# Graph-attention layer: where VectorE's mask and TensorE's scores stand in a step, and who adds the mask

## The reference

```python
h = relu(layernorm(x))                                   # x [4096, 256]
neib_att = tanh(neigh @ Wn1 + bn1) @ Wn2 + bn2           # [4096, 32]
x_att    = tanh(h @ Wx1 + bx1) @ Wx2 + bx2               # [4096, 32]
value    = neigh @ Wv + bv                               # [4096, 128]
ws = leaky_relu(x_att @ neib_att.T, 0.01)                # [4096, 4096]
ws = where(adj > 0, ws, -9e15); ws = softmax(ws, axis=1)
out = x + concat([h @ Wfx + bfx, ws @ value], axis=1)
```

## Time and profile before

| | |
|---|---|
| median of 3 runs | 552.23 us (551.5 to 552.99) |
| time of the profiled execution | 552.71 us, its span 550.5 us |
| granted TensorE clock over the span | 0.983 |
| PE busy | 505.3 us, 92% |
| DVE busy | 478.2 us, 87% |
| ACT busy | 432.7 us, 79% |
| POOL busy | 211.8 us, 38% |
| HBM read and written | 154 GB/s over the span |

### The profile page before, as it was taken

How to read it: one execution, slowest core, us unless ns; L and a number is a source line. 1 busy time by engine, 2 the same in 40 slices (tenths; PEclk the granted TensorE clock), 3 DMA queues, 4 the chain that set the end, 5 groups by cost and what they waited for, 6 DMA issues and landing times.

```text
span 550.5 us, 8742 instructions
## 1 busy us (share of the span) xinstructions
PE 505.3 (92%) x2759; PEld 378.3 (69%) x2759; DVE 478.2 (87%) x883; ACT 432.7 (79%) x585; POOL 211.8 (38%) x325
## 2 busy tenths in 40 slices
PE   5798788899999999999999999999999999998996
PEld 4455556677777767766877677766777686776784
DVE  2669897999999999999999999999998999996664
ACT  2563688898888888888888878888888889897553
POOL 1402123234633654355434553456435444440100
PEclk8898999899999999999999999999999999999999
DMA  7752865454456545664356445643565445620100
GB/s 205 190 166 48 143 135 98 92 115 78 76 87 139 89 69 96 117 135 76 59 107 147 73 78 113 119 91 64 95 114 96 77 74 94 113 46 1 40 1 19
DMA packets 38013, 52.00 MB, mean 94 GB/s; under 512 B 3920, under 2 KB 29776, under 8 KB 37968
## 3 DMA queue, kind: packets, MB, share of 16 engines
q0 software_dynamic: 9216, 33.56, 37.5%
q1 hardware_dynamic: 28752, 17.90, 11.3%
HBM read 80.81 MB, written 4.19 MB: 154 GB/s over the span
## 4 chain that ended last, share of the span: by engine, by line
PE 34%; DVE 16%; issue 11%; ACT 11%; POOL 7%; DMA 3%; DVEq 1%; POOLq 0%; ACTq 0%
PE ps_turned L884 10%; POOL scores L421 6%; DVE pt_lo L655 5%; PE ps_scores L861 5%; PE ps_product L903 4%; PE ps_product L905 4%; PE ps_product L904 4%; ACT scores L512 4%; ACT scores L524 4%; DVE mask L642 4%; DVE scores L676 3%; PE ps_scores L860 3%; DMA adj_in<-in_adj 3%; ACT pt_hi L489 2%; PE ps_product L814 1%
## 5 line engine op out<-in xcount | busy, mean ns | idle before, releaser
L421 POOL TENSOR_TENSOR scores<-scores,mask 128x512 f32<-128x512 f32 x109 | 129.2, 1186 | 203.6 <-ACT scores L512 203.6
L655 DVE TENSOR_TENSOR pt_lo<-ps_turned,pt_hi 128x512 fp32r<-128x512 f32 x256 | 175.1, 685 | 32.1 <-ACT pt_hi L489 15.9
L489 ACT ACTIVATE pt_hi<-ps_turned 128x512 fp32r<-128x512 f32 x256 | 152.5, 597 | 55.6 <-PE ps_turned L884 49.5
L884 PE MATMUL ps_turned<-ident,scores 128*128 128x128 f32 x1024 | 158.3, 277 | 11.4 <-DVE pt_lo L655 11.0
L884 PEld LDWEIGHTS ps_turned<-ident,scores 128*128 128x128 f32 x1024 | 119.9, 141 | 61.3 <-DVE pt_lo L655 30.4
L512 ACT ACTIVATE scores<-ps_scores 128x1024 f32<-128x1024 f32 x128 | 131.1, 1025 | 28.7 <-PE ps_scores L861 25.9
L524 ACT ACTIVATE scores<-scores,neg_top 128x2048 f32<-128x2048 f32 x64 | 127.9, 1998 | 0.0
L676 DVE CUSTOM_DVE_ANT_0 scores<-ps_scores,scores,top 128x1024 f32<-128x1024 f32 x96 | 122.2, 1273 | 2.8 <-ACT scores L512 0.9
L903 PE MATMUL ps_product<-pt_hi,v_hi 128*128 128x512 f32 x256 | 113.1, 442 | 0.2 <-DVE pt_lo L655 0.2
L861 PE MATMUL ps_scores<-neib,xs 128*128 128x512 f32 x256 | 109.9, 507 | 0.0
L905 PE MATMUL ps_product<-pt_lo,v_hi 128*128 128x512 f32 x256 | 101.4, 396 | 0.0
(11 more groups left out here) (76 smaller groups left out, 385.1 us busy)
## 6 DMA issues: line engine op xcount, KB each, us to landing
adj_in<-in_adj POOLq DMA_DIRECT2D x64, 512.0 KB, 5.5
scores<-in_L_gnn_neigh SPq DMA_DIRECT2D x8, 512.0 KB, 4.3
x_rows<-in_x SPq DMA_DIRECT2D x8, 512.0 KB, 6.6
x_left<-in_x SPq DMA_DIRECT2D x8, 256.0 KB, 5.7
x_right<-in_x SPq DMA_DIRECT2D x8, 256.0 KB, 2.9
out_h<-x_left SPq DMA_DIRECT2D x8, 256.0 KB, 2.3
out_h<-x_right SPq DMA_DIRECT2D x8, 256.0 KB, 5.1
scores<-in_x SPq DMA_DIRECT2D x1, 512.0 KB, 5.0
```

Of the source, the lines that this page charges most:

```text
L421: pool.tensor_tensor(half, half, mask[:, s % 2, BANK:CHUNK], ALU.add).then_inc(masked, 1)
L489: act.activation(pt_hi[:, (2 * b + u) % HI_RING], pt[:, u], ACT.Copy).then_inc(hi_done, 1)
L655: dve.tensor_tensor(pt_lo[:, u], pt[:, u], pt_hi[:, (2 * b + u) % HI_RING].bitcast(FP32), ALU.subtract).then_inc(lo_done, 1)
L884: last = pe.transpose(pt[:, u, i * P:(i + 1) * P], scores[:, parity * TILES + i, n * P:(n + 1) * P], ident[:, :])
```

## The change

VectorE makes the masks two chunks ahead instead of one, in a ring of three buffers instead of two, and from step 19 as the last thing of its step. What was behind `lo(s, 1)` (negated maximum, sums, outputs, side work) now stands between the two `lo`. TensorE's scores come first in its step, ahead of `turn(s, 0)`. From step 19 no mask matmul is left: GpSimd adds both halves, as two instructions of 512 columns. The adjacency loads go out on even steps, with a wait for the same masks as before. The ring of `pt_hi` has three buffers instead of four. ScalarE's copy of a finished group comes ahead of `hi(s, 0)`. The last loop of SyncE that was not written out is written out.

```diff
-HI_RING = 4
+HI_RING = 3
+MASK_RING = 3
...
-        mask = sb("mask", [P, 2, CHUNK], BF16)
+        mask = sb("mask", [P, MASK_RING, CHUNK], BF16)
...
@@ GpSimd
-                    pool.wait_ge(risen, s + 1 + PERIOD * it)
-                    half = scores[:, parity * TILES + tile, c * CHUNK + BANK:(c + 1) * CHUNK]
-                    pool.tensor_tensor(half, half, mask[:, s % 2, BANK:CHUNK], ALU.add).then_inc(masked, 1)
-                n = s - LOAD + 1 + ADJ_RING
+                    pool.wait_ge(risen, s + 1)
+                    pool.wait_ge(mask_done, s + 1)
+                    for h in range(2):
+                        half = scores[:, parity * TILES + tile, c * CHUNK + h * BANK:c * CHUNK + (h + 1) * BANK]
+                        last = pool.tensor_tensor(half, half, mask[:, s % MASK_RING, h * BANK:(h + 1) * BANK], ALU.add)
+                    last.then_inc(masked, 1)
+                n = s - LOAD + 2 + ADJ_RING
                 if n % LOAD == 0 and ADJ_RING <= n < STEPS:
-                    pool.wait_ge(mask_done, s + 1 + PERIOD * it)
-                    load_adj(n, n // CHUNKS + 2 * TILES * it)
+                    pool.wait_ge(mask_done, n - ADJ_RING + LOAD)
+                    load_adj(n, n // CHUNKS)
...
@@ ScalarE
+            def step(s):
+                aggregate(s)
+                hi(s, 0)
+                rise(s)
+                hi(s, 1)
+                power(s)
+                side(s)
...
@@ VectorE
-                if it_is(it, e, NEIGH_GROUPS - 1):
-                    mask_of(0, 0)
+                if e == NEIGH_GROUPS - 1:
+                    for n in range(2):
+                        mask_of(n)
...
-                if n >= 2:
-                    dve.wait_ge(scored, k - 1)
-                if n - 2 >= POOL_MASKS:
-                    dve.wait_ge(masked, k - 1 - POOL_MASKS)
+                if n >= MASK_RING:
+                    dve.wait_ge(scored, n - MASK_RING + 1)
+                if n - MASK_RING >= POOL_MASKS:
+                    dve.wait_ge(masked, n - MASK_RING + 1 - POOL_MASKS)
...
+            def step(s):
+                if s < POOL_MASKS:
+                    mask_of(s + 2)
+                leak(s)
+                lo(s, 0)
+                negate(s)
+                close(s)
+                x_work(s)
+                lo(s, 1)
+                if POOL_MASKS <= s < STEPS - 2:
+                    mask_of(s + 2)
+                neigh_rest(s)
...
@@ TensorE
-                on_pool = h == 1 and s >= POOL_MASKS
+                on_pool = s >= POOL_MASKS
...
-                turn(s, 0, it)
-                score(s, 0, it)
-                score(s, 1, it)
-                product(s, -2, it)
+                score(s, 0)
+                score(s, 1)
+                turn(s, 0)
+                product(s, -2)
```

More of the change, by code:

```diff
@@ L206, in build @@
         block = ctx.enter_context(nc.Block())
[L209 to L215, removed]
         def wait(engine, semaphore, value):
-            if not isinstance(value, int) or value > 0:
+            if value > 0:
                 engine.wait_ge(semaphore, value)
-        def main(engine, step):
-            for s in range(END):
-                step(s, 0)
         def x_due(s, stage):
@@ L295, in _ @@
                     b2_in, 16)
[L296 to L299, removed]
+            for e in range(2, NEIGH_GROUPS):
+                sp.wait_ge(turned, KT * (e - 1))
+                load_neigh(e)
             for side, w, b, w_in, b_in in ((1, w_fx, b_fx, wfx, bfx), (0, w_v, b_v, wv, bv)):
@@ L334, in step @@
                         load_x_right(g + 1)
-            main(sp, step)
+            for s in range(END):
+                step(s)
             sp.wait_ge(right_done, GROUPS)
@@ L476, in _, with hi @@
             act.wait_ge(consts_in[0], CONSTS_IN[0])
-            encode(act, neigh_step)
-            def hi(s, u, it):
+            for e in range(NEIGH_GROUPS):
+                neigh_step(e)
+            def hi(s, u):
                 b = s - BACK_LAG
@@ L531, in step @@
                     if e := x_due(s, X_TURN + k):
[L532 removed]
+                        x_turned_copy(e, k, x_bank(e))
                 if e := x_due(s, X_TANH):
[L534 to L536 removed]
+                    x_tanh(e, x_bank(e))
+            def step(s):
+                aggregate(s)
[4 more added lines that the diff above has]
+                side(s)
+            for s in range(END):
+                step(s)
         @block.vector
@@ new lines, in leak @@
+                if not 0 <= n < STEPS:
+                    return
+                parity, tile, c = chunk_of(n)
+                cols = scores[:, parity * TILES + tile, c * CHUNK:(c + 1) * CHUNK]
+                dve.wait_ge(risen, n + 1)
+                if n >= POOL_MASKS:
+                    dve.wait_ge(masked, n + 1 - POOL_MASKS)
+                if c:
+                    dve.wait_ge(leaked, n)
+                start = top[:, tile % 2, c - 1:c] if c else -3.0e38
+                if c == 0 and n >= 2 * CHUNKS:
+                    dve.wait_ge(top_done, n // CHUNKS - 1)
@@ new lines, in leak, with negate @@
+                dve.sem_inc(joined, 1)
+                dve.tensor_tensor_reduce(cols, ps[:, n % 2], cols, SLOPE, start, ALU.add, ALU.max,
+                                         top[:, tile % 2, c:c + 1]).then_inc(leaked, 1)
+            def negate(s):
+                n = s - 1
+                if not 0 <= n < STEPS or n % CHUNKS != CHUNKS - 1:
+                    return
+                dve.wait_ge(leaked, n + 1)
+                if n >= 2 * CHUNKS:
+                    dve.wait_ge(exp_done, (n // CHUNKS - 1) * HALVES)
+                dve.tensor_scalar(neg_top[:, n // CHUNKS % 2, :], top[:, n // CHUNKS % 2, CHUNKS - 1:CHUNKS],
+                                  -1.0, None, ALU.mult).then_inc(top_done, 1)
@@ L941, in step @@
                         value_layer(value_due(s - h), h)
-            main(pe, step)
+            def step(s):
+                score(s, 0)
+                score(s, 1)
+                turn(s, 0)
+                product(s, -2)
+                turn(s, 1)
+                product(s, -1)
+                agg_turn(s)
+                side(s)
+            for s in range(END):
+                step(s)
 INPUTS = ["x", "adj", "L0_gnn_neigh", "L0_gnn_Wx1", "L0_gnn_bx1", "L0_gnn_Wx2", "L0_gnn_bx2", "L0_gnn_Wn1",
```

234 lines of the change are left out of this document (105 added, 129 removed).

## The result

The changed kernel takes 559.94 us (median of 4 runs, 558.38 to 562.67) against 551.87 (4 runs, 548.46 to 552.99): ratio 1.016, 95% interval 1.010 to 1.023. It is slower by 8 us, clear of the noise, where I forecast 4 us less. 559.94 lies in the stated range; the direction is wrong, and it is next to the 562 of the rival "shut out".

What follows compares the result with a forecast made beforehand. VectorE and TensorE, both 96% busy, were taken as the bound, then the new cycle. -6.1 us over 99 steps and +2.0 in the last ten gave -4.1: 548 us predicted, range 532 to 565.

Steps and rivals of the forecast that it cites:

- shut out: Rival: both GpSimd adds keep VectorE's mask out at its step's end; 573 us, 562 at half price; chance 0.27.
- Costed at nothing: Reordering effects given no time: early masks, scores first, side work between the lo, rings, loads, SyncE's loop.
- Scores first: TensorE's scores can go once an earlier leak is done and are past before turn may start; no loss.
- The new cycle: Way from leak over scores, rise and two adds to the next leak sets the pace; case's chance 0.42.
- T: Average step time, 4T covering four steps: 3.58 us with side work, 3.43 in the last ten steps.
- Hindrance of the mask: A mask holding up GpSimd's second half: 0.26 us in the cycle, 0.26 in the pair's other step.
- From the add to the leak: Semaphore time between GpSimd's last add and VectorE's leak: some 0.05 us.
- GpSimd's side work and loads: Loads behind an add and GpSimd's side work start the next add late: estimated 0.1 us in four steps.
- The bare cycle: The four-step sum of 14.33 us without the mask's hindrances: 10.36 for the chain, 3.15 VectorE's step, small extras.
- The bounds: Mask beside two adds: from nothing lost to 0.75 us more every step; 0.26 taken, near the lower end.
- The miscounted leak: The stage before was counted as leak 18 to leak 117, 99 steps of 3.642 us.
- Freed: Rival: the cycle has slack, only VectorE's and TensorE's work counts; T about 3.4, 528 us; chance 0.17.

Runs made afterwards that it cites:

- e2: The changed kernel with the second add taken back: TensorE masks the first half by matmul, GpSimd adds only the second; 526.73 us, ratio 0.956 to the kernel before.
- e11: The changed kernel with GpSimd adding the second half only and nobody masking the first from step 19 on; 518.69 us, ratio 0.941 to the kernel before.
- e3: The changed kernel with ScalarE's rise ahead of its first copy (hi) of the step; 543.12 us, ratio 0.987 to the kernel before.
- e5: e2 with ScalarE's rise first, as in e3; 539.41 us, ratio 0.979 to the kernel before.
- e8: e2 with TensorE's turn ahead of the scores again; 538.13 us, ratio 0.977 to the kernel before.
- e7: e2 with VectorE's mask back in mid-step behind the first lo, still two chunks ahead; 546.73 us, ratio 0.994 to the kernel before.
- e6: The changed kernel with VectorE's mask replaced from chunk 22 on by similarly long statistics not seen to wait for GpSimd; 548.38 us, ratio 0.995 to before.
- e12: The changed kernel with GpSimd's two adds of 512 columns made one of 1024; 552.31 us, ratio 1.002 to the kernel before.
- e14: The changed kernel with one add of the last 768 columns, the first 256 left unmasked; 529.46 us, ratio 0.962 to the kernel before.
- e9: The changed kernel with GpSimd's side work (reciprocal square roots, bias adds) left out after the first groups; 549.14 us, ratio 0.998 to the kernel before.
- e13: The changed kernel with the edits of e6, e3 and e9 together; 528.88 us, ratio 0.963 to the kernel before.
- e10: The changed kernel with the edits of e6 and e3 together; 532.21 us, ratio 0.966 to the kernel before.

## Why the prediction was wrong

The change is three things that I summed to -4 us, and each was far larger: the order gives 24 us (e2 against before), the matmuls' absence 8 (e11 against e2), the second add takes 41 (the change against e11). These are prices in this order of undoing them; e3 against e5 shows that another order gives others.

*Costed at nothing, the step that failed for the gain.* "Scores first ... no loss" was given no gain either, and e8 measures 11 us with one add. Of the mask moved to the end I charged a new hindrance and credited nothing, though the earlier trace rows had shown that 0.33 us a step was to be had by standing clear of the add; e7 measures 20 us, part of it perhaps the same as e8's. That VectorE loses 0.33 us a step to the add was right, and it is what the order took back with one add in the way.

*The new cycle, the step that failed for the sign.* It was the right mechanism (e3, e6, e12 and e14 fit it) and too small. I had T = 3.58 and 3.43; measured were 3.73 and 3.56, some 16 us over the stage. Its terms:

- Hindrance of the mask: 0.26 + 0.26 in 4T, 0.13 us a step, 14 us. e6 measures 11.6. This size was right; the count was not complete, since the layer norm's scaling went from 0.40 to 0.71 us as well.
- From the add to the leak: 0.05 us for the semaphore. Measured are 0.17 us where the leak waits for the add, 0.12 more in 4T, some 3 us in all (an estimate).
- GpSimd's side work and loads: 0.1 in 4T, less than 3 us in all. e9 measures 10.8. With two adds GpSimd has 91 us of waiting for the rise left instead of 204, so its own work between two adds comes in the way more often. That is four times the term, part of it through the masks; with the mask harmless and the rise first it is 3.3 us (e13 against e10), about what I had.
- The bare cycle: with the mask's 0.52 taken out of 14.33 it gives 3.45 us a step; e6's leaks of chunks 19 and 117 (101.33 and 459.21) are 3.65 apart. Of this 0.2, the 0.03 of the semaphore are shown, and up to 0.1 can be the side work just named; the rest, some 0.1 a step or 8 to 10 us, stays open. I summed stretches end to end for one pattern of two steps; the side work of TensorE and ScalarE meets it at changing places, which such a sum leaves out. That this is the cause was argued, not shown.

*The bounds.* I took the hindrance "near the lower end" because the leak would wait for the same add. In the stage of two adds the masks take 0.72 us on average, 0.30 more than undisturbed, so the guess was near. The upper end and more occur (2.26 us above), in one step of a group.

*The miscounted leak.* With 98 steps of 3.68 my own sum would have read about 545 instead of 548, farther off; it did not hide the cause.

*The rivals.* "Shut out" had the time, 562 at half its price, but not the reason, so its nearness is luck: the mask's part of the shutting out is 12 us of 41 (e6), e12, in which the mask is shut out for longer, is faster, and its sign, a mask's mean over 0.95 us, did not come (0.67). Its condition, the add ending more than 2.4 us after the leak, is met (3.95 us at 268.56). "Freed" describes e2, not the change. The Trainium skill (SBUF — State Buffer, "SBUF: two separate sides") has an exclusive lock for the whole instruction; the masks of these traces that met an add agree, down to the 8-column mask that waited 2.02 us. What I took from it, that both adds shut the mask out, came true for 5 masks of 22.

*What was to be seen.* Right: 38 mask matmuls, TensorE at 88%, POOL near 340 us (333), waits for the mask gone, a mask near 0.7 us, over 3.4 in the last ten steps, VectorE waiting for the add ahead of the leak (11.9 us in 300), no waits for loads in the middle (0.5 us in all). Wrong: leaks 3.5 to 3.6 apart.

## What to carry to other kernels

A change that moves work to an idle engine and reorders the rest is several changes: undo one at a time, since here a gain of 32 us and a loss of 41 hid in a result of 8. An idle engine's share says nothing when its work lies on the way between two others: ask what the longer operation does to the round trip, and what else that engine must fit between. An operation that another engine's work holds up is worth placing clear of it, and the place has to be looked for again when that work grows: the same place gave masks of 0.43 us beside one add and 0.67 beside two.

## What the hardware showed beyond that

- A mask of 8 columns, 0.15 us undisturbed, took 2.02 us beside two adds and a bias add in a row: what is held up depends on the kind of operation, not on its size. Statistics over 256 float32 columns on the same engine were not held up at all (0.417 us on average in e13, beside 218 adds).
- Between two GpSimd adds issued in a row VectorE sometimes gets in (a mask of 0.53 us at 267.01 in the changed kernel, the pair stretched to 2.48 us) and sometimes not (2.26 us at 251.49); both times it had begun 0.16 to 0.24 us before the first add's end. In the changed kernel it got in 17 times and not 5 times; what decides stays open.
- A leak that waits for GpSimd's add starts 0.17 us after the add's end (268.56 to 268.73 in the changed kernel).
- GpSimd's add of a bf16 mask to float32 scores took 1.16 us for 512 columns, 1.655 for 768 and 2.146 for 1024: about 0.98 us for 512 columns more, and 0.18 us for each instruction (an estimate from the three).
